# A state-space layer's preparation steps placed anew among its scans, and decays set to zero through a step of 1e30

## What is computed

```python
xz = x @ W_in.T;  xp, z = split(xz)
xc = silu(causal_conv(xp, conv_w) + conv_b)            # 384 channels
dt, Bt, Ct = split(xc @ W_xproj.T)
dt = softplus(dt @ W_dt.T + b_dt);  A = -exp(A_log)    # A: 384 x 16
# for each token t of a sequence, from h = 0:
dA = exp(dt_t[..., None] * A)
h = dA * h + (dt_t * x_t)[..., None] * B_t[:, None, :]
y = einsum('bdn,bn->bd', h, C_t)
# behind the scan:
y = (y + xc * D_param) * silu(z);  return y @ W_out.T
# the layer: 0.5 * (mamba(x) + mamba(x reversed) reversed), on a layer norm of h, added to h
```

## Time and profile before

| | us |
|---|---|
| median of 3 runs | 4795.98 (4794.58 to 4800.1) |
| the profiled execution | 4795.38 |
| its span (first to last instruction) | 4793.6 |
| state-space layer, from about 1216 to 3886 in the span | 2670 |
| one steady group, forward and backward half | 85.24 + 82.40 |

### The profile page before, as it was taken

One profiled execution on the slowest core, in us unless ns is written; L12 is line 12 of the kernel. 1 busy time (PEld: TensorE's weight loads), 2 busy tenths in 40 slices (PEclk: granted clock), 3 DMA queues, 4 the chain that ended last, 5 costly groups with the idle time before them and its releaser, 6 DMA issues. The chain is left out here.

```text
span 4793.6 us, 70708 instructions
## 1 busy us (share of the span) xinstructions
PE 3905.7 (81%) x20800; PEld 2516.5 (52%) x20800; DVE 3303.5 (69%) x5112; ACT 2480.3 (52%) x5040; POOL 3113.2 (65%) x1637
## 2 busy tenths in 40 slices
PE   7999986996887878787787788778787775999994
PEld 4666644663454454445444444544454543666673
DVE  5677763111798989999999999999999986111114
ACT  3555542222576766767676676767667643222221
POOL 3222212441898999999999999899999951444441
PEclk9999997997898989998899988989999877999997
DMA  1000012342333333333333333333333321333456
GB/s 34 20 20 23 16 62 60 110 133 77 102 110 112 113 114 116 111 116 112 119 104 114 116 115 112 111 116 106 114 116 111 115 81 32 114 111 118 125 168 216
DMA packets 267120, 478.89 MB, mean 100 GB/s; under 512 B 39404, under 2 KB 176444, under 8 KB 266908
## 3 DMA queue, kind: packets, MB, share of 16 engines
q1 hardware_dynamic: 235776, 403.02, 26.4%
q0 software_dynamic: 28032, 73.17, 6.1%
q10 hardware_dynamic: 3100, 0.64, 0.1%
HBM read 409.75 MB, written 41.81 MB: 94 GB/s over the span
## 5 line engine op out<-in xcount | busy, mean ns | idle before, releaser
L1822 POOL TENSOR_TENSOR m_xh<-m_u,m_Bb 128x1536 f32<-128x1536 f32 x512 | 1767.0, 3503 | 163.9 <-PE bank L1737 118.3
L1791 DVE TENSOR_TENSOR_SCAN bank<-bank,m_xh 128x512 f32<-128x512 f32 x960 | 1153.7, 1215 | 98.3 <-ACT bank L1778 98.3
L1778 ACT ACTIVATE bank<-m_dt,m_Ac 128x508 f32<-128x508 f32 x1536 | 1025.5, 682 | 25.8 <-DVE m_xh L1791 25.8
L1737 PEld LDWEIGHTS bank<-ident,m_xh 128*128 128x128 f32 x6144 | 744.8, 150 | 311.8 <-issue 228.9
L1737 PE MATMUL bank<-ident,m_xh 128*128 128x128 f32 x6144 | 839.6, 288 | 47.8 <-POOL m_xh L1811 40.7
L1811 POOL TENSOR_TENSOR m_xh<-m_xh,m_Cb 128x1536 f32<-128x1536 f32 x192 | 665.9, 3468 | 63.1 <-DVE m_xh L1791 62.1
L1791 DVE TENSOR_TENSOR_SCAN m_xh<-bank,m_xh 128x512 f32<-128x512 f32 x576 | 682.6, 1208 | 27.2 <-ACT bank L1778 22.9
L1802 DVE TENSOR_TENSOR m_xh<-bank,m_Cb 128x512 f32<-128x512 f32 x960 | 644.0, 671 | 2.6 <-DMA m_Cb<-BC_rows 2.6
L1580 PE MATMUL bank<-m_xp,m_dg 128*128 128x512 f32 x768 | 389.9, 654 | 105.1 <-ACT m_xc L1588 94.7
L1204 ACT ACTIVATE f1t_h<-bank,f1t_b 128x512 f32<-128x512 f32 (+1 forms) x276 | 147.9, 587 | 509.8 <-PE bank L1234 509.8
L1777 ACT COPY bank<-m_none 128x4 f32<-128x4 f32 x992 | 159.4, 161 | 421.4 <-DVE m_xh L1802 311.7
(11 more groups left out here) (370 smaller groups left out, 6461.5 us busy)
## 6 DMA issues: line engine op xcount, KB each, us to landing
m_Bb<-BC_rows SPq DMA_DIRECT2D x256, 512.0 KB, 4.9
m_Cb<-BC_rows SPq DMA_DIRECT2D x256, 512.0 KB, 4.0
f1t_w<-f_w SPq DMA_DIRECT2D x46, 576.0 KB
m_r<-m_dt POOLq DMA_DIRECT2D x32, 768.0 KB, 7.4
f1t_w1a<-f_w SPq DMA_DIRECT2D x46, 384.0 KB
f0t_w<-f_w SPq DMA_DIRECT2D x22, 576.0 KB
f1c_yg<-rows_y SPq DMA_DIRECT2D x16, 768.0 KB, 8.3
f1t_w1b<-f_w SPq DMA_DIRECT2D x92, 96.0 KB
```

Source lines behind the costliest of these rows:

```text
L1737: mm = pe.matmul(bank[:, c, sl], xh[n % NX][:, c, sl], K.ident[:, :], is_transpose=True, start=False, stop=(d == 1 and n == NS - 1), skip_ ...
L1778: act.activation(o[:, :, lo:hi], seqs(dt[d][:, c, :])[:, :, lo:hi], ACT.Exp, scale=Ac[:, c, n:n + 1]).then_inc(s_dA, 1)
L1791: dve.tensor_tensor_scan(o, bank[:, RING[d][p], way], xh[n % NX][:, c, way], 0.0, ALU.mult, ALU.add).then_inc(s_h, 1)
L1822: pool.tensor_tensor(xh[n % NX][:, :, :], u[d][:, :, :], Bb[q % RB][:, n % QN, :].unsqueeze(1).to_broadcast([P, DC, TOK]), ALU.mult).then_ ...
```

## The change

Two things change. The table `POS` gets other numbers for nearly every part. And the zero decays are made another way: `act_sp` copies only the 127 columns of each sequence that need a step, and behind its first copy one more copy puts 1e30 from a new tile `far` into the edge columns of all three tiles of `dt`. `exp(1e30 * A)` with negative A is zero, so one exponential of 512 columns writes the whole decay, and no copy of zeros stands before it. `u` is computed from PSUM and sees nothing of this. Of the table the diff shows the rows that the text speaks of most; a pair of numbers holds the part for d = 0 and d = 1, a triple the three channel tiles, and a name that ends in 0 or 1 the half that is prepared.

```diff
-            "y": (6, 7, 9), "pe_yT": (8, 9, 11), "act_yT": (10, 11, 13), "pe_D0": (14, 15, 17), "pe_D1": (6, 16, 25), "pe_out": (17, 18), "out": (14, 15),
...
-            "pe_sp0": (26, 36, 40), "act_sp0": (30, 39, 41), "u0": (34, 38, 41), "pe_sp1": (32, 38, 42), "act_sp1": (34, 38, 40),
-            "u1": (32, 37, 40),
+            "y": (5, 8, 9), "pe_yT": (7, 11, 15), "act_yT": (10, 11, 14), "pe_D0": (11, 12, 20), "pe_D1": (8, 12, 20),
+            "pe_out": (16, 18), "out": (14, 16), "act_rows": (9, 12), "rows": (9, 11), "stats": 16, "rstd": 19, "norm": 35,
...
+            "act_w1": (25, 25), "act_ln": (27, 29), "pe_sp0": (24, 32, 35), "act_sp0": (35, 37, 40), "u0": (33, 37, 40),
+            "pe_sp1": (33, 36, 40), "act_sp1": (36, 39, 41), "u1": (35, 38, 41),
...
-        none = sb("none", [P, G])
+        far = sb("far", [P, DC, G])
...
-                dve.memset(none[:, :], 0.0)
+                dve.memset(far[:, :, :], 1.0e30)
...
             def act_sp(act, c):
                 act.wait_ge(s_spps, s * DC + c + 1)
-                act.copy(dt[d][:, c, :], bank[:, front(c), :]).then_inc(s_sp, 1)
+                lo, hi, edge = (1, P, 0) if d == 0 else (0, P - 1, P - 1)
+                act.copy(seqs(dt[d][:, c, :])[:, :, lo:hi], seqs(bank[:, front(c), :])[:, :, lo:hi]).then_inc(s_sp, 1)
+                if c == 0:
+                    ends = dt[d][:, :, :].rearrange("p c (b t) -> p c b t", b=G)[:, :, :, edge:edge + 1]
+                    act.copy(ends, far[:, :, :].unsqueeze(3)).then_inc(s_edge, 1)
...
         def act_decay(act, g, d, p):
             n, c = divmod(p, DC)
-            lo, hi, edge = (1, P, 0) if d == 0 else (0, P - 1, P - 1)
-            o = seqs(bank[:, RING[d][p], :])
             back, db, pb = before_in_bank(d, p)
             if p == 0:
                 act.wait_ge(s_sp, (g * 2 + d + 1) * DC)
+                act.wait_ge(s_edge, g * 2 + d + 1)
...
-            if back or pb // DC not in BY_POOL[d] or d == 0 and p == ROWS_TO:
-                act.copy(o[:, :, edge:edge + 1], none[:, :].unsqueeze(2))
-            act.activation(o[:, :, lo:hi], seqs(dt[d][:, c, :])[:, :, lo:hi], ACT.Exp, scale=Ac[:, c, n:n + 1]).then_inc(s_dA, 1)
+            act.activation(bank[:, RING[d][p], :], dt[d][:, c, :], ACT.Exp, scale=Ac[:, c, n:n + 1]).then_inc(s_dA, 1)
```

More of the change, by code:

```diff
@@ L1367, in mamba_phase @@
         POS = {
-            "y": (6, 7, 9), "pe_yT": (8, 9, 11), "act_yT": (10, 11, 13), "pe_D0": (14, 15, 17), "pe_D1": (6, 16, 25), "pe_out": (17, 18), "out": (14, 15),
-            "act_rows": (11, 13), "rows": (12, 14), "stats": 14, "rstd": 18, "norm": 40,
[3 rows of a table removed]
-            "act_pj": (15, 10), "act_xc": (14, 8), "act_e": (23, 23), "act_w1": (23, 26), "act_ln": (26, 29),
-            "pe_sp0": (26, 36, 40), "act_sp0": (30, 39, 41), "u0": (34, 38, 41), "pe_sp1": (32, 38, 42), "act_sp1": (34, 38, 40),
-            "u1": (32, 37, 40),
+            "y": (5, 8, 9), "pe_yT": (7, 11, 15), "act_yT": (10, 11, 14), "pe_D0": (11, 12, 20), "pe_D1": (8, 12, 20),
+            "pe_out": (16, 18), "out": (14, 16), "act_rows": (9, 12), "rows": (9, 11), "stats": 16, "rstd": 19, "norm": 35,
[3 rows of a table added]
+            "act_dt1": (18, 20, 22), "pe_pj": (11, 10), "act_pj": (15, 11), "act_xc": (14, 8), "act_e": (24, 22),
+            "act_w1": (25, 25), "act_ln": (27, 29), "pe_sp0": (24, 32, 35), "act_sp0": (35, 37, 40), "u0": (33, 37, 40),
+            "pe_sp1": (33, 36, 40), "act_sp1": (36, 39, 41), "u1": (35, 38, 41),
         }
@@ L1432, in mamba_phase @@
             sem(n) for n in ("dA_ready", "dBx_ready", "h_ready", "read_by_dve", "read_by_pool", "summed"))
-        s_copied = sem("rows_in_psum")
+        s_copied, s_edge = sem("rows_in_psum"), sem("edges_set")
         s_er, = ctx.software(K, 1)
```

## The result

The changed kernel takes **4650.73 us** (median of 4 runs, 4649.06 to 4653.99), the kernel before 4796.95 us beside it: a ratio of 0.9696, interval 0.9679 to 0.9712. The forecast was 4688 us, 107 us faster; 146 us came. That is near the low end of the forecast's range (4645 to 4752) and is the time of rival (a), 4653 us, but the rival's reason is wrong, as the experiments show.

The account below looks back on a forecast made before the run. VectorE was taken as the bound, with about 14.5 us of standing still per 167.6 us group, mostly waiting for ScalarE's held-up steps. Waits removed 164 less 57 added gave 107 us, so 4688 us, range 4645 to 4752.

Parts of the forecast that it names:

- rival (a): ScalarE's pause at the loop's turn is a data wait, so scan 3 has no new wait: 4653 us, chance 0.07.
- charge of 35 us: Forward half, after the loop's turn: new wait of 2.7 us before scan 3, queued behind conv 1, 13 times.
- gate product: VectorE's wait for TensorE's state sums before this product, 14.6 us; about 1 us a time was to stay unchanged.
- all 69.7 us: VectorE's 31 waits for ScalarE's step copies before `u`, counted as removed entirely by the new places.
- rival (c): TensorE's softplus sums stay the bound, 2 us later than forecast, giving back 62 us: 4750 us, chance 0.13.
- 67.5 us: VectorE's waits for decays before scans that write PSUM: 98.3 less 15 x 2.05 us, counted as gone.
- burst at step 15: Backward half: VectorE's 2.05 us wait for a decay stays, less 0.2 us for two copies, 15 groups, 3 us.
- 6 us charged for steps 23 to 26: ScalarE is denser at these steps: an added wait of 0.35 us x 16.
- the pause stays: ScalarE's 4.23 us idle at the loop's head is the jump's instruction fetch and remains, however little ScalarE has to do.
- thin covers: Several covers are only 0.2 to 0.4 us; charged 1 us a group, 15 us in all.
- (b): GpSimd becomes the bound, the product of state 8 getting its buffer late: 29 us lost, 4717 us, chance 0.16.
- (d): Steps 11 to 20, first half: TensorE's granted clock falls, projections double, 128 us lost against 107 won: 4816 us, chance 0.09.

Follow-up runs that it names:

- the padded kernel: The changed kernel with one empty semaphore instruction on ScalarE ahead of each decay that had had an edge copy (62 a group): 4712.25 us, ratio 0.9813.

## Why the prediction was right, and where not

- **The direction, and what goes** were right by the steps given. The rows that the forecast named lost 126.6 us, net of new waits, against 164; the other 14.6 of the 141.2 us are the gate product, which it had left alone. That the time still came out 37 us under the forecast is no merit of the sum: a charge of 35 us never arose and the gate product went unforeseen, and the two outweigh what fell short. The failed size is `u`: I had all 69.7 us going, and 18.9 stay, at one place, the second `u` of the forward half. My working counted VectorE's and ScalarE's time up to `u1`'s first part and took the others for covered. The trace of after shows why that one isn't. TensorE's three pairs of products, the first and then the second:

```profile
2061.95 1.10 PE L1667 MATMUL bank<-m_u,ident 128*128 128x512 f32 x2 [1.20 <-ACT m_gz L1569]
...
2069.81 2.07 PE L1667 MATMUL bank<-m_u,ident 128*128 128x512 f32 x2 [3.73 <-DVE m_u L1680]
```

  and VectorE behind the second:

```profile
2075.95 0.69 DVE L1680 TENSOR_TENSOR m_u<-bank,m_xc 128x512 f32<-128x512 f32 x1 [2.24 <-ACT m_dt L1673]
```

  The second set stands idle 3.73 us for the first `u` and then runs at a granted clock of 0.50:

```profile
2069.70:2075.20 5.50, 5.39 (x7) 2.16 (x8) 4.01 (x5) 0.88 (x2) 5.50 (x3) 0.50 0.27 111
```

  This is rival (c)'s mechanism, at one of six places. The slow pair of before stood in the first set; now it stands in the second.
- **Decays before scans.** 67.5 us were to go, 50.5 went. The burst at step 15 of the backward half stays as forecast, 1.87 us (2.05 less 0.2). New is a wait of 0.52 us at step 9 of that half, 14 times: its conv 1 comes two steps earlier and waits 1.84 us for TensorE. I had priced that move at 0.1 us, 1.5 us in all; it is 7.6 us.

```profile
2103.37 0.69 ACT L1588 ACTIVATE m_xc<-bank,m_cb 128x512 f32<-128x512 f32 x1 [1.84 <-PE bank L1580]
2104.76 1.23 DVE L1792 TENSOR_TENSOR_SCAN bank<-bank,m_xh 128x512 f32<-128x512 f32 x1 [0.52 <-ACT bank L1779]
```

  The 6 us charged for steps 23 to 26 came, in the forward half: there scans 23 and 26 wait 3.9 us each over the layer, 6.7 us more than before (0.08 and 0.15 us in a steady group, the rest in groups 0 and 15). Scan 4 of the backward half waits 0.2 us a group, 2.9 in all.
- **The step that failed is "the pause stays".** I had a choice between two readings of ScalarE's 4.23 us, a jump or data, and took the jump, rightly: no data wait explains it, and in the padded kernel the whole chain up to scan 3 comes, with 3.5 us a turn for 2.7. But I took the jump's price as fixed, "however little ScalarE has left to do". It hangs on the length of the body, and the edit that I had priced at 3 us, the copies, shortens the body past the step: 364 records to 306, 4.6 to 4.9 us to 0.26. That turned +35 us into nothing. My sign for rival (a), no wait at scan 3, came true with (a) false, so it couldn't tell a data wait that was resolved from a jump that had become cheap.
- **The gate product.** I left its 14.6 us where they were. It took both changes to remove them: 6.1 us are back in the padded kernel and 5.0 stand in the one with new places and copies, 6.4 in the one with old places and no pause. That TensorE's convolution no longer runs late and slow ahead of it is the likely reason, but no run shows that link by itself.
- **The sum.** 141.2 and 6.2 us of busy time make the layer's 147.6. My 107 falls short of it by the 35 for scan 3 and the 14.6 at the gate product that I had kept, and by the 6.2 of busy time, together 55.8; against it stand the 18.9 us of `u`, the 7.6 at step 9 and the 3.8 that stay at the projections, together 30.3 instead of the 16.5 charged for thin covers and conv 1. 107 + 55.8 - 13.8 = 149, against the 147.6 of the layer; smaller rows on either side I haven't sorted. With the pause, the forecast's 4688 stands against 4712 us.
- **Rivals.** (a) gave the time and not the reason. (b) doesn't hold yet, as the written-out loop shows; it is near: GpSimd idles 0.6 us in a forward half. (c) is true at one place. (d) doesn't hold: the granted clock of the layer rose from 0.89 to 0.93, and the projections in the emptied stretch take 2.21 and 2.22 us, as before:

```profile
2031.83 2.21 PE L1765 MATMUL bank<-m_wo,m_r 128*128 128x192 f32 x12 [1.43 <-ACT m_r L1754]
2034.81 2.22 PE L1765 MATMUL bank<-m_wo,m_r 128*128 128x192 f32 x12 [0.77 <-DVE H L1835]
```

  The pauses there are 1.43 and 0.77 us, under the 1.5 that I had found, and the granted clock of the stretch (2031.8 to 2037.1) is 1.00.

## What to carry to other kernels

A pause at the head of a loop that no data explains may be a price of the jump, and that price can have a step in the length of the body: count each engine's instructions from one turn to the next, and look at the row of instruction fetches, before an edit is priced at "so many instructions of 0.1 us". Here 17 instructions that do nothing are worth 60 us, and writing out one engine's loop won 23. Where a pause is charged to a jump, ask also whether the edit in hand changes the jump. And a wait in a tuned order is often the cover of something later: before it is filled with other work, follow what starts from the step that is pushed back.

## What the runs showed that was not expected

- ScalarE's jump back takes 0.26 to 0.28 us with 306 or 323 records in the loop and 4.6 to 5.5 us with 340, 364 or 368. Moving the body, by 45 instructions for 306 and by 96 for 364 and 368, changed nothing. VectorE's takes 2.8 to 3.1 us with 356 and didn't change with 100 instructions ahead of it. GpSimd (120 records) and SyncE (102) take 0.25 to 0.31 us in every run, and TensorE, with 724 records, 0.27 to 0.38 us.
- The fetch row tells the state without the records: 172 to 174 packets (1.41 to 1.43 MB) with both pauses, 106 or 107 (0.87 or 0.88 MB) with VectorE's alone. With VectorE's loop written out and no pause left it is

```profile
q14 instruction: 63, 0.52, 0.0%
```

- The pause costs nearly its whole length, although ScalarE, which makes it, is busy only two thirds of the layer (1693 of 2522 us): some 4.6 us more of pause a turn became 62 us over 13 turns, 4.7 us each. ScalarE's lead was what let the convolution be done in time; without it TensorE idled 5.04 us and then took 5.96 us for it instead of 3.72.
